# One tile in every fourth group of the relation pass, fetched row by row by ScalarE's own DMA queue

## The reference, cut to what matters

```python
loop_message = h @ loop_weight
xw = jnp.einsum('ni,rio->rno', h, W)                  # 8 relations
msg = xw[rel, src] + bias_term[rel]                   # one row of 128 per edge
gate = jax.nn.sigmoid(jnp.sum(msg * gw[rel], axis=-1) + gate_bias[rel, 0])
agg = jax.ops.segment_sum(msg * gate[:, None], dst, num_segments=n_nodes)
return jax.nn.relu(agg + loop_message)
```

## Time and profile before

| | |
|---|---|
| median of three runs | 4851.01 us |
| profiled execution | 4856.42 us |
| its span | 4854.6 us |
| mean granted TensorE clock | 0.697 of full speed |
| TensorE busy | 3016.2 us (62%) |
| VectorE busy | 2483.6 us (51%) |
| ScalarE busy | 1327.0 us (27%) |
| GpSimd busy | 3239.6 us (67%) |

### The profile page before, as it was taken

The page is one execution under the profiler, slowest core; times in us unless marked ns, Lnnn a source line. Parts: engine busy times, 40 slices in busy tenths (PEclk is TensorE's granted clock), DMA queues, the critical chain, the costliest instruction groups (busy, mean ns, idle before and its releaser), DMA issues. The chain is left out here.

```text
span 4854.6 us, 53090 instructions
## 1 busy us (share of the span) xinstructions
PE 3016.2 (62%) x15318; PEld 2692.3 (55%) x15318; DVE 2483.6 (51%) x4658; ACT 1327.0 (27%) x3623; POOL 3239.6 (67%) x3391
## 2 busy tenths in 40 slices
PE   3777677776677777777383333333345776777762
PEld 3666666664567677766343333333345666666661
DVE  3444444445799999997671111111134444444447
ACT  0000000002699999997450000000011000000003
POOL 4777777772677777775017777777746777777761
PEclk7665666656899999998695555555576666666665
DMA  4344444431444444442052222222214444444430
GB/s 130 109 109 109 109 110 112 109 105 45 133 119 119 119 119 119 119 119 85 14 214 53 53 53 53 53 53 53 53 29 122 109 109 109 109 109 111 111 82 27
DMA packets 249279, 458.28 MB, mean 94 GB/s; under 512 B 104966, under 2 KB 147208, under 8 KB 249000
## 3 DMA queue, kind: packets, MB, share of 16 engines
q0 software_dynamic: 119808, 280.51, 22.8%
q1 hardware_dynamic: 129192, 174.48, 11.0%
HBM read 411.70 MB, written 43.03 MB: 94 GB/s over the span
## 5 line engine op out<-in xcount | busy, mean ns | idle before, releaser
L783 POOL DMA_INDIRECT rows<-gat_table,src_i x1664 | 1573.3, 946 | 531.8 <-issue 531.8
L971 PE MATMUL p_adc<-adw,hot_t 128*128 128x8 f32 x3328 | 655.8, 335 | 558.2 <-DVE hot_t L809 558.0
L783 POOL DMA_INDIRECT rows<-rel_table,rel_i x832 | 786.4, 945 | 313.5 <-issue 247.8
L971 PEld LDWEIGHTS p_adc<-adw,hot_t 128*128 128x128 f32 x3328 | 638.4, 294 | 629.4 <-DVE hot_t L809 628.5
L783 POOL DMA_INDIRECT rows<-mlp_table,src_i x832 | 788.4, 948 | 264.7 <-issue 264.7
L1004 PE MATMUL p_sum<-hot,rows 128*128 128x128 f32 x1664 | 384.3, 425 | 669.8 <-issue 643.5
L991 PE MATMUL p_sum<-rows,hot 128*128 128x133 f32 x3328 | 759.1, 417 | 4.2 <-DVE rows L832 4.2
L1004 PEld LDWEIGHTS p_sum<-hot,rows 128*128 128x128 f32 x1664 | 359.3, 328 | 695.4 <-issue 695.4
L991 PEld LDWEIGHTS p_sum<-rows,hot 128*128 128x128 f32 x3328 | 714.7, 318 | 5.2 <-DVE rows L832 5.2
L998 PE MATMUL p_sum<-hot,rows 128*128 128x128 f32 x3328 | 458.1, 303 | 232.0 <-ACT rows L949 231.9
L998 PEld LDWEIGHTS p_sum<-hot,rows 128*128 128x128 f32 x3328 | 438.5, 216 | 272.8 <-ACT rows L949 272.8
(11 more groups left out here) (207 smaller groups left out, 3301.0 us busy)
## 6 DMA issues: line engine op xcount, KB each, us to landing
drow<-in_dst_rows SPq DMA_DIRECT2D x208, 512.0 KB
rows<-gat_table,src_i POOLq DMA_INDIRECT x1664
rel_table<-tab SPq DMA_DIRECT2D x49, 512.0 KB, 2.6
rows<-mlp_table,src_i POOLq DMA_INDIRECT x832
eat<-in_edge_t SPq DMA_DIRECT2D x104, 128.0 KB
rows<-rel_table,rel_i POOLq DMA_INDIRECT x832
gat_table<-tab SPq DMA_DIRECT2D x14, 479.5 KB, 4.7
mlp_table<-tab SPq DMA_DIRECT2D x7, 896.0 KB, 4.1
```

The source lines that it names most:

```text
L783: pool.indirect_dma_start(out=rows[:, st.slot, t, :], out_offset=None, in_=table[:, :], in_offset=bass.IndirectOffsetOnAxis(ap=of[:, st.gr ...
L971: last = nc.tensor.matmul(p_adc[k][:, t, 0:2 * H], hot_t[:, k, t * P:(t + 1) * P], adw[:, half, :], start=True, stop=True)
```

## The change

In groups 3, 7, 11, ..., 103 of the relation pass, 26 of 104, GpSimd fetches seven tiles and leaves out the eighth (`t` = 7). For that tile SyncE reads the 128 indices from `rel_index` in DRAM into one row on partition 0 (`idx_row`, two buffers), and ScalarE loads them to registers, 32 at a time, and issues one DMA for each row of the table: 128 DMAs of 512 B, each to one partition of the tile. They count on one of two semaphores `by_row`, each DMA by 16. TensorE waits for seven gathers and for the 128 rows of that group. The attention and MLP passes keep their programs; the wait for the gathers is only written through a helper (`arrived`).

```diff
+BY_ROWS = 4
@@ edge_pass
         if rel:
+            idx_row = s.sb("idx_row", [1, 2, P], I32)
+            row_index, by_row = [s.row_index0, s.row_index1], [s.by_row0, s.by_row1]
             p_sum = [s.ps(f"p_sum{k}", [P, 512]) for k in range(2)]
+        def by_rows(st, fast):
+            return rel and fast and st.n % BY_ROWS == BY_ROWS - 1
+
+        def arrived(eng, st, fast):
+            many = sum(T - by_rows(Step(m, 0, 0, 0, 0, None), fast) for m in range(st.n % RING, st.n + 1, RING)) if fast else (st.visit + 1) * T
+            wait(eng, s.gathered[st.slot], many * 16)
+            if by_rows(st, fast):
+                eng.wait_ge(by_row[st.n // BY_ROWS % 2], (st.n // BY_ROWS // 2 + 1) * 16 * P)
@@ SyncE, load
+                if by_rows(st, fast):
+                    visit = st.n // BY_ROWS
+                    wait(sp, s.rows_read, visit - 1)
+                    sp.dma_start(idx_row[:, visit % 2, :], net.rel_index[:, st.group:st.group + 1, T - 1].rearrange("p g -> g p")).then_inc(row_index[visit % 2], 16)
@@ GpSimd, gather
-                for t in range(T):
+                for t in range(T - by_rows(st, fast)):
@@ ScalarE
+            def gather_rows(st, fast):
+                if not by_rows(st, fast):
+                    return
+                visit = st.n // BY_ROWS
+                wait(act, s.summed, st.n - depth(fast, RING) + 1)
+                act.wait_ge(row_index[visit % 2], (visit // 2 + 1) * 16)
+                for q in range(0, P, 32):
+                    _, at = nc.values_load_multi_w_load_instructions(idx_row[0:1, visit % 2, q:q + 32], engines=[mybir.EngineType.Activation], min_val=0,
+                                                                     max_val=sh.NP * R - 1, skip_runtime_bounds_check_because="an index of the table")
+                    for j, v in enumerate(at):
+                        last = act.dma_start(rows[q + j:q + j + 1, st.slot, T - 1, :], table[bass.ds(v, 1), :])
+                        last.then_inc(by_row[visit % 2], 16)
+                act.sem_inc(s.rows_read, 1)
@@ ScalarE, program
+                if rel:
+                    if fast:
+                        drive(act, sh, [(of(gather_rows), [0])], fast)
+                    return
...
-            if not rel:
-                pick(act, net, program)
+            pick(act, net, program)
@@ TensorE, add_up of the relation pass
-                    pe.wait_ge(s.gathered[st.slot], (st.visit + 1) * 16 * T)
+                    arrived(pe, st, fast)
```

More of the change, by code:

```diff
@@ L687, in edge_pass @@
              "messages", "summed", "sums_copied", "sums_turned", "added", "edge_product", "pre",
-             "scaled", "hidden", "index_in", "w1e_zero", "deviation", "onehot_rest", "pool_passed", "sp_passed"]
+             "scaled", "hidden", "index_in", "w1e_zero", "deviation", "onehot_rest", "pool_passed", "sp_passed",
+             "row_index0", "row_index1", "by_row0", "by_row1", "rows_read"]
     width = TAB if gat else HID if mlp else F
@@ L764, in _ @@
                 sp.dma_start(beta[:, :], a["L1_gnn_be1"].partition_broadcast(P)).then_inc(s.weights_in, 16)
-            pick(sp, net, lambda fast: drive(sp, sh, [(lambda st: load(st, fast), [0])], fast))
+            with nc.allow_non_contiguous_dma(reason="the indices of one tile in a row"):
+              pick(sp, net, lambda fast: drive(sp, sh, [(lambda st: load(st, fast), [0])], fast))
         def operands(fast):
@@ L814, in logits @@
                 dve.wait_ge(s.adc_gathered, st.n + 1)
-                dve.wait_ge(s.gathered[st.slot], (st.visit + 1) * 16 * T)
+                arrived(dve, st, fast)
                 wait(dve, s.weights_ready, st.n - depth(fast, 2) + 1)
```

## The result

The changed kernel takes 5329.6 us (median of four runs, 5327.7 to 5332.0) against 4851.4 us: ratio 1.0985, 95% interval 1.0966 to 1.1004, so 478 us slower. The forecast was slower by 1071 us, 5922, with a range from 5460.

A forecast was written before the change was run, and what follows sets the result against it. GpSimd's gathers were taken to bound the relation pass, then ScalarE's 26 visits of 68.5 + 12.5 + 0.1 = 81.1 us, 2109 us in all: +1071 us, 5922 us on the median. The range was 5460 to 6560 us, holding 0.85.

The forecast's parts named there:

- What bounds the kernel, and who takes over: Relation pass: GpSimd paces it at 1.25 us a gather; after the change ScalarE's 26 visits set the pace.
- V: Time of one ScalarE visit in the relation pass (waits, value loads, 128 row DMAs, increment), forecast at 81.1 us.
- A row: ScalarE's issue of one row DMA with its address work, priced from SyncE's window fetch: 0.535 us, 68.5 us for 128.
- The lower bound of a row: Least time for ScalarE to issue one row with its address work: 0.19 + 0.298 = 0.49 us.
- The values: ScalarE's loads of 32 indices to registers: 0.09 us each further value, 3.1 us a batch, 12.5 us a visit.
- Rival 2: ScalarE's value loads each cost a whole load: V = 105 us, total 6544 us; chance 0.15, with the skill's price.
- Sum: ScalarE's visit: 68.5 + 12.5 + 0.1 = 81.1 us; 26 of them 2109 us, kernel +1071 us.
- Start and tail: Relation pass: ScalarE begins some 2.4 us after GpSimd's start; landing, matmuls and add after the last issue take 6.6 us.
- the first, the cheap end: Rival on ScalarE's visit: loads nearly free, row DMA as cheap as the cheapest; V = 64.1 us, total 5481; chance 0.15.
- The other side, ScalarE keeping up: Rival in the relation pass: V below 39.9 us, GpSimd still the bound, -32.5 us, total 4818.5; chance 0.08.
- Rival 4: Landings in the relation pass: rows land one after the other, 1.4 us or more each; V = 180 us, total near 8490; chance 0.05.
- The issue rule: ScalarE's row DMAs: against the skill's rule, issue is five times the packet; the new queue costs far more than 32.5 us saved.

## Why the prediction was wrong

- **What bounds the kernel, and who takes over.** Right. GpSimd paced the pass with 1.25 us a gather; the pass is the larger of 806 x 1.25 and 26 V. Five lengths of the visit bear it out: 31.4 and 38.3 us under 38.8 (every fourth group) and 58.2 under 58.75 (every sixth) gave the gain of the gathers left out, within 3 us; 58.2, 62.1 and 65.6 us at every fourth group gave 5330, 5430 and 5526 us, where 4851 + 26 V - 1040 is 5324, 5426 and 5517.
- **A row: the step that failed.** The prediction says "A row is so 0.19 + 0.343 = 0.535 us". Measured: 0.157 + 0.213 = 0.370. The 343 ns belong to a DMA of 128 pieces over 128 partitions. I saw that the rows here are one piece on one partition, and took the price of the register address over that of the shape; the register address costs its own two instructions of 37 and 29 ns and some 30 ns behind each, and makes the DMA itself no longer. 128 x 0.165 = 21.1 us of the 22.9 us by which the visit was too long.
- **The lower bound of a row.** Also wrong. I built 0.49 us from 298 ns, a static DMA of one piece, and from SyncE's gap of 0.19. Three single DMAs at 298, 392 and 518 ns bound nothing from below: in a run of equal ones it is 213. Wrong too is the sentence "Even the cheapest DMA with no address work at all (0.298 and some 0.04 to the next) is above 0.31 us": fixed rows follow one another every 0.294 us, and that version gains.
- **The values.** A batch takes 2.24 us and not 3.1, since a further value is 0.059 us in place of 0.09: 3.5 us a visit too much. The estimate of the Trainium skill, "Runtime: NRT & Kernel Launch", section "Instruction fetch mechanics" (about 200 ns a register in bulk, from HBM), does not carry over to loads from SBUF: 0.059 us here. Rival 2 fell with it.
- **Missing.** The first DMA of ScalarE after a load takes near 0.45 us in place of 0.213, 0.9 us a visit. And ScalarE's queue pauses for some 0.31 us in place of 0.03 after every 128 of its instructions, three times a visit, another 0.9 us. With 128 x 0.3694 = 47.3 us and 9.0 us of loads this is 58.1 of the 58.2 us.
- **Sum.** 26 x (81.1 - 58.2) = 595 us, the distance from 5922 to the 5330 measured. Start and tail were right within 2 us.
- **The rivals.** The nearest was the first, the cheap end (V = 64.1, 5481); the truth lay beyond it. The other side, ScalarE keeping up, needed V = 39.9 us, and at 58.2 it missed by 18 us a visit. Rival 4 fell: TensorE started 1.3 us behind the last DMA instruction, and a DMA is 0.213 us.
- **The issue rule.** The Trainium skill, "DMA: Bandwidth & Descriptors", section "Issuing engines are not separate DMA queues", says that a second issuing engine saves only sequencer time, which is usually small beside the DMA. In these runs it is not small: the sequencer's time was the bound (58.2 us a visit), and sharing it between two queues made the pass 33 us shorter than before, where one queue made it 474 us longer.

## What to carry to other kernels

Price a queue by a run of the very DMA that it will issue: going from one row to sixteen moved the instruction from 0.22 to 0.32 us, and single ones among others bound nothing. When work moves from a bound engine to an idle one, compare the idle engine's whole visit with the bound engine's time between visits: under it the gain is the work moved, over it the whole stage takes the new engine's pace. The same 128 rows were 10% slower on one queue at every fourth group, and 0.4% and 0.6% faster at every sixth, or split over two queues. At every sixth group a visit had 0.55 us to spare; on the chips whose queues pause, the same two versions were 10% and 7% slower than the kernel before.

## What the runs showed of the hardware

- A DMA instruction at a fixed address takes longer (265 ns) than the same at a register address (213 ns), though the pair of register instructions makes the latter dearer in all, 0.370 against 0.294 us. The fixed ones also follow one another faster (0.03 us between two against 0.16), and no run separates the two.
- ScalarE's queue pauses after every 128 of its instructions, whatever they are: 79 times in the pass of the changed kernel, some 0.31 us between two instructions in place of 0.03. One queue of the kind "instruction" (q14) grows from 156 packets to 236, 80 more, and moves 8192 bytes in one; behind each of the 79 pauses such a packet starts 1.0 to 1.4 us later. That a fetch of instructions causes the pause is likely and not shown.
- The first row DMA after a load of values takes near 0.45 us on ScalarE and some 0.26 us on SyncE, against 0.213 and 0.220 for the others.
- TensorE does its 1664 records in 254 us in place of 384, with a mean clock of 0.58 in place of 0.59. The four groups of a visit come at once behind its 49 us wait:

```profile
3008.30:3012.00 3.70, 3.67 (x19) 3.70 (x20) 0.00 (x0) 0.00 (x0) 0.00 (x0) 0.55 0.04 5
3012.00:3017.60 5.60, 5.54 (x48) 5.15 (x46) 4.53 (x6) 0.00 (x0) 3.77 (x4) 1.00 0.15 38
3020.00:3060.00 40.00, 0.00 (x0) 0.00 (x0) 0.00 (x0) 0.00 (x0) 23.60 (x25) 0.52 0.18 44
```

These are windows of the changed kernel within one visit. The granted clock is 0.55 (the 1.2 GHz level, nearly all of it) for the first 3.7 us of work, 1.00 (2.4 GHz) for the next 5.6 us, and 0.52 in the idle time behind. In the kernel before, groups come evenly, 3.7 us of work in each 10. There the clock rises too, but behind the work; one group and the idle time after it:

```profile
3004.00:3007.70 3.70, 3.56 (x16) 3.49 (x16) 0.00 (x0) 0.00 (x0) 2.79 (x4) 0.50 0.22 53
3007.90:3011.00 3.10, 0.00 (x0) 0.00 (x0) 1.51 (x2) 0.00 (x0) 2.49 (x3) 1.00 0.24 63
```

So the nearly equal mean clocks hide that the later groups of a burst run at 1.00 and the evenly spaced groups of the kernel before at 0.50. It buys nothing here, as TensorE is not the bound.
